# Two attention steps and a normalising stage, moved from stages of their own into the dense passes before them

## The reference, cut to what matters

```python
query, key = (x @ Wq + bq).reshape(n, 2, 128), (x @ Wk + bk).reshape(n, 2, 128)   # 2 heads
qs, ks = query / norm(query), key / norm(key)
terms = [x0]                                        # x, for both heads
for _ in range(4):
    prev = terms[-1]
    gcn = segment_sum(prev[row], col) * deg_inv     # neighbours' mean
    kvs = einsum('lhm,lhd->hmd', ks, prev)
    attn = (einsum('nhm,hmd->nhd', qs, kvs) + prev.sum(0)) / (qs . ks.sum(0) + n)
    terms.append(0.5 * gcn + attn)
x = layernorm(x + (concat(terms) @ Wo + bo) / 2)
```

## Time and profile before

| what | value |
|---|---|
| median of 3 runs (lowest, highest) | 5326.28 us (5324.18, 5327.95) |
| profiled execution, its span | 5325.0 us |
| PE, PEld busy over the span | 81%, 57% |
| DVE, ACT, POOL busy | 53%, 27%, 61% |
| DMA | 909 MB, mean 171 GB/s |
| second dense pass, from 2758.3 us to 3222.0 us | 463.6 us |
| step two, to 3301.6 us | 79.6 us |
| third dense pass, to 3764.2 us | 462.6 us |
| step three, to 3862.3 us | 98.1 us |
| fourth dense pass, to about 4196 us | 334 us |
| normalising stage, to 4279.6 us | 84 us |

### The profile page before, as it was taken

The page is one execution under the profiler, slowest core; times in us unless marked ns, Lnnn a source line. Parts: engine busy times, 40 slices in busy tenths (PEclk is TensorE's granted clock), DMA queues, the critical chain, the costliest instruction groups (busy, mean ns, idle before and its releaser), DMA issues. The chain is left out here.

```text
span 5325.0 us, 78049 instructions
## 1 busy us (share of the span) xinstructions
PE 4321.5 (81%) x26640; PEld 3018.0 (57%) x26640; DVE 2815.1 (53%) x7430; ACT 1451.2 (27%) x2914; POOL 3251.7 (61%) x3382
## 2 busy tenths in 40 slices
PE   4677866979868787788879997999889767777786
PEld 3444434545535556554446664666555467667775
DVE  6588886755367776535562315221432444455554
ACT  1377850010057664111120102010210122222222
POOL 2766626767767775075516661776177367777774
PEclk6789988989989999699989998999999898999998
DMA  4265559999933344195588887988697465555553
GB/s 145 45 61 80 91 100 194 199 182 187 202 80 101 104 126 109 60 289 159 168 265 271 270 248 250 280 268 253 228 303 241 130 171 144 143 149 146 151 153 82
DMA packets 1261118, 909.00 MB, mean 171 GB/s; under 512 B 446403, under 2 KB 1181934, under 8 KB 1260638
## 3 DMA queue, kind: packets, MB, share of 16 engines
q1 hardware_dynamic: 909866, 519.09, 39.3%
q0 software_dynamic: 102704, 232.38, 16.1%
q10 hardware_dynamic: 248132, 152.25, 9.9%
HBM read 696.10 MB, written 118.89 MB: 153 GB/s over the span
## 5 line engine op out<-in xcount | busy, mean ns | idle before, releaser
L1687 PE MATMUL ps<-adj_d,xs_d 128*128 128x464 bf16 (+1 forms) x4704 | 992.8, 367 | 60.1 <-DVE xs_d L1648 60.1
L3166 POOL DMA_INDIRECT rows_mg<-p_tab,src_idx x784 | 758.3, 967 | 273.4 <-issue 238.1
L1601 POOL DMA_INDIRECT rows_d<-xh_tab,src_idx x632 | 617.7, 977 | 479.8 <-POOLq L187 207.4
L1601 POOL DMA_INDIRECT rows_d<-x_tab,src_idx x512 | 499.1, 975 | 475.5 <-POOLq L187 264.4
L1687 PEld LDWEIGHTS ps<-adj_d,xs_d 128*128 128x128 bf16 x4704 | 466.1, 101 | 509.1 <-DVE xs_d L1648 61.9
L1295 POOL DMA_INDIRECT rows_d<-h_tab,slot_idx x490 | 497.0, 1014 | 266.9 <-issue 143.9
L2216 POOL DMA_INDIRECT rows_g<-x_tab,src_idx x444 | 434.2, 978 | 164.7 <-issue 127.3
L3263 PE MATMUL ps<-win_mg,turned_hot_mg 128*128 128x128 f32 x1568 | 341.2, 302 | 201.2 <-DVE pre_mg L3215 201.0
L1431 PE MATMUL ps<-adj_d,xs_d 128*128 128x512 bf16 (+1 forms) x2028 | 441.0, 375 | 54.6 <-DVE xs_d L1396 49.9
L1673 PEld LDWEIGHTS ps<-onehot_d,rows_d 128*128 128x128 f32 x3552 | 428.6, 192 | 66.6 <-DVE onehot_d L1619 33.5
L1673 PE MATMUL ps<-onehot_d,rows_d 128*128 128x72 f32 (+1 forms) x3552 | 421.4, 275 | 31.3 <-DVE onehot_d L1619 26.3
(11 more groups left out here) (442 smaller groups left out, 7541.4 us busy)
## 6 DMA issues: line engine op xcount, KB each, us to landing
adj_d<-adjacency SPq DMA_DIRECT2D x140, 812.0 KB
adj_d<-adjacency SPq DMA_DIRECT2D x84, 857.5 KB
attr_mg<-in_edge_attr SPq DMA_DIRECT2D x195, 256.0 KB
xp_g<-x_tab SPq DMA_DIRECT2D x70, 448.0 KB
k_rows_d<-k_tab ACTq DMA_DIRECT2D x56, 448.0 KB
loc_mg<-loc_rows SPq DMA_DIRECT2D x196, 128.0 KB
q_s<-q_tab SPq DMA_DIRECT2D x42, 448.0 KB
rden_s<-rden_tab SPq DMA_DIRECT2D x42, 448.0 KB
```

The source lines that it names most:

```text
L1601: nc.gpsimd.indirect_dma_start(rows[:, q % GR * K + k, :], None, table, bass.IndirectOffsetOnAxis(ap=src_idx[:, j:j + 1], axis=0)).then_in ...
L1687: last = nc.tensor.matmul(ps[:, m % 2, 0:w], xs[:, g * GW + k, e, :], adj[:, slot, k, 0:w], start=(g == 0 and k == 0 and e == 0), stop=(g ...
L3166: nc.gpsimd.indirect_dma_start(rows[:, q % RR, k, :], None, p_tab, bass.IndirectOffsetOnAxis(ap=src_idx[:, j:j + 1], axis=0)).then_inc(row ...
```

## The change

Steps two and three lose their stages. The pass itself goes through the nodes in 14 **visits** of 512 or 384 columns (`NODE_PARTS`), as soon as the sums of those columns are complete (`needs`). `fused_slots` writes the order: one **slot** for each dense tile, and some behind the last tile, each with at most one piece of `keys_values`, up to two groups, the tile, and a visit (`ask` ahead of the groups on PE, `finish` behind the tile). Pieces come one to a slot from the second slot on, where before one came to five tiles; visits may begin at slot 35. The two passes have 4 blocks a head instead of 5, so 56 tiles instead of 70, and gather 368 tiles of edges (92 groups) instead of 316 (79 groups). By the order, 9 visits stand beside tiles and 5 behind the last one, together with the last 8 groups. All loads and stores of a visit are issued by ACT; the loads of rden and share go into a single buffer, q into two. Buffers are those of `raw` and of the key rows. In pass two ACT first stores the whole `xT` to `x_kept`, for the passes' general fallback (a branch not taken here).

In pass four `ending_slots` puts two pieces into a slot, so `keys_values` and `LastAttention` end at slot 18, and the normalising stage (`LastNodes`, the same work as `layer2_last`) enters a visit at every second tile from slot 19 on; 11 enter beside tiles, 3 behind them, and the last is through 6 slots later. There, too, `xT` is stored to `x_kept` first, and DVE may change `xT` only when that is done.

Cut to its core:

```diff
-SPLITS = {1: Split(6, 490, 528), 2: Split(5, 464, 468)}
+SPLITS = {1: Split(6, 490, 528), 2: Split(4, 464, 416)}
...
+        def fused_slots():
+            slots, visits, ready = [], [], [(c, nw * P) for c, nw in NODE_PARTS]
+            clock, t, q, p, finished = 0.0, 0, 0, 0, 0
+            free_at = order.index((blocks, G - 1)) + 1
+            while t < tiles or q < groups or finished < PARTS_N:
+                took = pieces[p:p + 1] if t else []
+                opens = p >= len(pieces) and t >= free_at
+                p += len(took)
+                group = []
+                while q < groups and len(group) < 2 and clock > 4.5 + GATHER_US * (q + 1):
+                    group.append(q)
+                    q += 1
+                tile = t if t < tiles else None
+                able = [v for v in ready if needs(*v)[1] <= q and (needs(*v)[0] < 0 or stored_at(needs(*v)[0]) < t or tile is None)]
+                ask = finish = None
+                if opens and able:
+                    ask = len(visits)
+                    visits.append(able[0])
+                    ready.remove(able[0])
...
                     def _(pe):
-                        for t in range(tiles + 1):
-                            beside(nc.tensor, t)
-                            for q in gathered[t]:
+                        for s, slot in enumerate(slots):
+                            beside(nc.tensor, slot)
+                            if step:
...
+                                if slot.ask is not None:
+                                    step.ask(pe, slot.ask, finished)
+                            for q in slot.groups:
...
+                            if slot.finish is not None:
...
+                                step.finish(pe, slot.finish, turn_bank(slot))
...
+                def start(self, act):
+                    if keeps:
+                        act.dma_start(x_kept, xT[:, 0:NP]).then_inc(self.kept, 16)
...
+                def load_rest(self, act, i):
...
+                        if i:
+                            act.wait_ge(self.made, HEADS * i)
+                        act.dma_start(self.share[:, 0:w], dinv_row[c:c + w].partition_broadcast(P)).then_inc(self.rest_in, 16)
+                        for h in range(HEADS):
+                            act.dma_start(self.rden[h][:, 0:w], rden_tab[h * P:(h + 1) * P, c:c + w]).then_inc(self.rest_in, 16)
...
+                def ask(self, eng, i, finished=0, again=False):
...
+                        for h in range(HEADS):
+                            nc.tensor.matmul(ps[:, 4 + h, 0:w], kv[:, h, :], self.q[i % 2][h][:, 0:w], start=True, stop=True).then_inc(self.asked, 1)
+                    elif eng is nc.vector:
+                        eng.wait_ge(self.rest_in, 16 * (1 + HEADS) * (i + 1))
...
+                        nc.vector.tensor_tensor(a, a, self.share[:, 0:w].unsqueeze(1).to_broadcast([P, HEADS, w]), ALU.mult).then_inc(self.scaled, 1)
...
+        class LastNodes:
...
+            def begin(self, act, again=False):
...
+                    act.dma_start(x_kept, xT[:, 0:NP]).then_inc(self.kept, 16)
...
+            def on_vector(self, line, ready):
...
+                    dve.wait_ge(self.kept, 16)
+                    nc.vector.tensor_tensor(x, x, a, ALU.add).then_inc(self.final, 1)
...
-            if step < ORDER:
-                layer2_step(step)
-        layer2_last()
+        layer2_step(1)
+        for step, table, to, sums in ((2, xh_tab, xh2_tab, G), (3, xh2_tab, xh_tab, PARTS_N)):
+            make = fused_step(step, to, step == 2)
+            dense_pass(f"2{step}", table, HEADS, SPLITS[HEADS], [[keys_values(table, HEADS, 1, sums)]], make)
...
+        dense_pass(f"2{ORDER}", x_tab, 1, SPLITS[1], [[keys_values(xh_tab, HEADS, 2, PARTS_N)], [LastAttention]], ending=LastNodes)
```

More of the change, by code:

```diff
@@ L45 @@
 BATCH = 14
+NODE_PARTS = [(g * GC + half * BLOCK, GW - BW if half else BW) for g in range(G) for half in range(2)]
+PARTS_N = len(NODE_PARTS)
+Slot = namedtuple("Slot", "pieces groups tile ask finish")
+TILE_US, GROUP_US, GATHER_US, PIECE_US, VISIT_US = 4.2, 1.75, 5.05, 1.6, 4.3
 MOST = 256
@@ L1508, in dense_pass @@
-                    for k, piece in enumerate(pieces):
-                        before = phases[opened.index(k) - 1] if k and k in opened else ()
-                        due[1 + k * (tiles - 1) // len(pieces)].append((before, piece))
-                    gathered = [[] for t in range(tiles + 1)]
-                    for q in range(groups):
-                        gathered[min(tiles, 2 + q * tiles // groups)].append(q)
-                    def beside(eng, t):
-                        for before, piece in due[t]:
+                            for k in range(most):
+                                pieces.append([(work, k, g) for work in phase if work.parts == most] +
+                                              [(work, 0, g) for work in phase if work.parts < most and k == most // 2])
@@ new lines, in dense_pass, with stored_at, needs @@
+                    pieces = [(phases[opened.index(k) - 1] if k and k in opened else (), piece) for k, piece in enumerate(pieces)]
+                    def stored_at(m):
+                        return order.index((m + 1, 2) if m else (1, G - 1)) if m < heads * blocks - 1 else tiles
+                    def needs(c, w):
+                        first_block = (heads - 1) * blocks
+                        covering = [first_block + b for b in range(blocks) if b * block_of < c + w]
+                        g = c // GC
+                        of_dense = c + w <= blocks * block_of
+                        sums = 0 if of_dense else groups if g == G - 1 else max(0, FINAL[g] - tail // K)
+                        return covering[-1] if c < blocks * block_of else -1, sums
@@ new lines, in dense_pass @@
+                    if step:
+                        slots, visits = fused_slots()
+                        step.visit(visits)
+                        begins = min(k for k, slot in enumerate(slots) if slot.ask is not None)
+                    elif last_nodes:
+                        slots, visits = ending_slots()
+                        last_nodes.visit(visits)
+                        begins = min(k for k, slot in enumerate(slots) if slot.ask is not None)
+                    else:
+                        slots = even_slots()
@@ L1518, in beside @@
+                    first_idle = min(k for k, slot in enumerate(slots) if slot.tile is None)
+                    def beside(eng, slot):
+                        for before, piece in slot.pieces:
                             for work in before:
@@ L1638, in add @@
                             nc.vector.tensor_tensor(a, a, sums_of(q), ALU.add).then_inc(added, 1)
[L1640 to L1642 removed]
+                        for k, slot in enumerate(slots):
+                            if slot.tile is not None and splits_at(slot.tile) is not None:
+                                h, g = splits_at(slot.tile)
                                 s = h * G + g
```

683 lines of the change are left out of this document (502 added, 181 removed).

## The result

The changed kernel took **5374.93 us** (median of 4 runs, 5361.89 to 5384.15) against 5325.23 us for the kernel before (4 runs, 5323.53 to 5327.95) in the same session: a ratio of 1.009 (95% interval 1.0077 to 1.0104), so slower by some 50 us. Forecast were 5275 us, 5200 to 5350, with a chance of 0.16 for slower by over 0.2%. The forecast missed its range and its sign. The profiled execution has a span of 5382.4 us; it was the slowest of the four.

What follows compares the result with a forecast made beforehand. PE was taken to bound passes two and three, no engine the three stages. Gains of 131 us made 5325 into 5194; new DMA waits of 81 us left a gain of 50: 5275 us, range 5200 to 5350.

Steps and rivals of the forecast that it cites:

- The sum without new waits: Steps two and three and pass four fused: gains of 50, 46 and 35 us, together 131, giving 5194 us.
- The waits for pieces: PE waiting for the loads of pieces: 15 us each in passes two and three, 17 in pass four.
- the starved queue: Rival: piece loads stay at 84 GB/s on ACT's queue, 91 us a pass, 5427 us; 0.16, shared with waits over 142 us.
- the volume alone: Rival: only bytes count, waits at their floors of 9, 9 and 17 us, 5229 us; chance 0.20.
- the uncovered chain: DVE's part of visits behind the last tile, covered by nothing: 3 us for the first visit, 4 for the last.
- late loads: Visits' `load_rest` into one buffer, 0.79 MB after `made`: 0 to 30 us a pass, 8 taken.
- The passage: From a fused pass's last store to the next stage: 4 us.
- Pass four: With the normalising stage inside: 383 us against 417.8 before waits, gain 35; some 410 us with waits.
- The tiling: Passes two and three with 56 tiles and 92 groups: PE's work 411 us, 35 less a pass.
- The rivals: Only volume counts, 5229 us, 0.20; ACT's queue starves, 5427, shared 0.16; visits behind late gathers, 5300 to 5337, no own chance.
- The slower rival: ACT's queue starves in passes two and three: 91 us of waits each, 5427 us; 0.16, shared with waits over 142 us.
- its point of 40 us a pass: Piece waits in passes two and three from which the slower rival decides: 3.1 us more to a slot.

Runs made afterwards that it cites:

- shifted_back: The changed kernel with 48 words (192 bytes) of each SBUF partition left empty ahead of the planes, no instruction changed: 5360.82 us, ratio 1.0059.
- before_shifted: The kernel before with 80 words (320 bytes) of each SBUF partition left empty ahead of the planes: 5339.58 us, ratio 1.0024.
- pieces_apart: The changed kernel with the 14 pieces of the second and third pass at every second tile, not at each: 5335.29 us, ratio 1.0014.
- q_early: The changed kernel with a visit's q loads given out once PE has asked with the buffer, value sums writing their own buffer: 5366.15 us, ratio 1.0091.
- no_fallback: The changed kernel with pieces at every second tile, early q loads and 48 empty words (5305.82 us), now without the fallback's node work: 5301.0 us, ratio 0.9934.
- five_blocks: The changed kernel with the old tiling, five blocks and 316 gathered tiles in passes two and three: 5394.81 us, ratio 1.0139.
- tiling_only: The kernel before with four blocks and 368 gathered tiles in passes two and three, nothing moved: 5368.12 us, ratio 1.0080.
- little_kept: The changed kernel with both stores of x_kept cut to 1/49 of their bytes: 5360.44 us, ratio 1.0074.
- both_little_kept: The changed kernel with pieces at every second tile, early q loads and 48 empty words (5305.82 us), now x_kept stores at 1/49: 5299.85 us, ratio 0.9934.

## Why the prediction was wrong

The profiled execution lies 107 us above the forecast, the median 100. By stages: the first pass 17, step one and what lies ahead 7, the second pass 35, the third 27, the fourth 20.

Two steps failed. "**The sum without new waits**" put the three moved stages too low: PE at the durations of an undisturbed pass, 50 us behind the last tile where there were 61, 4 us for a passage where there were 8 to 10, and no wait between the ending's pieces. And the first pass was left out of the sum without a reason.

*The first pass: a term that was missing.* "Only what is edited changes" was never written down, but the sum rests on it. The edit moved every buffer of the passes by 704 bytes, which costs 14 us in the first pass by `shifted_back` and 17 by `before_shifted`, 9 by the means of all kernels, and perhaps some in the fourth, 423.5 us in `shifted_back`. The second pass of `shifted_back`, 564.8 us, was not shorter.

*The waits for pieces: right in size; PE's work beside them was not.* Forecast were 15 us a pass plus 8 for `x_kept`; measured 12.8 + 6.7 us in the second pass and 18.2 in the third. DMA was at 0.99, as said, and the starved queue (91 us) and the volume alone (9 us) both fell. The sum priced PE at the durations of an undisturbed pass (4.12, 1.72, 1.56 us). With 9 of 14 visits that is some 436 us up to the end of the last tile of the second pass; PE was busy for 449.7. The clock behind waits is part of that, since `pieces_apart` has 10 us less there, though in the third pass it gave nothing back.

*Behind the last tile.* The sum gave the five visits their share of PE's work (5/14 of 58, 21 us), the eight groups 14, the uncovered chain 3 + 4 and late loads 8: 50 us. It took 61.2. PE's work was 45.4 us and not 35, at a granted clock of 0.80 (the eight groups alone 18 us), and the waits for q 12.7. The loads were late at q and not only at `rden`: in a slot behind the tiles the next q is loaded in the visit before's finish, and needed at once. I had said PE would idle ahead of L3109 for `made`; it idled 0.3 us there and 12.7 us ahead of L3083. Removing it alone brought little, because `rden` is the next in line (`q_early`).

*The passage.* "4 from the last store to the next stage" was read behind a step. As I read the program, a fused pass has at its end both the wait for its last stores and the branch that used to stand between pass and step, and it jumps over longer code (only this part is shown, by `no_fallback`): 9.9, 8.3 and 8.3 us, 14 in all over the forecast.

*Pass four.* The waits for loads (18.5 us against 17) and the chain behind the last tile (28.8 us from its end to the last store, against 26) were right. The sum lacked PE's waits for DVE between dependent pieces of the attention, 9.1 + 3.8 us and more; before, a tile lay between any two. They did not decide, though: spread out, the pass grew by 8 us.

*The tiling* was rightly a gain inside the fused pass: against `five_blocks` 32 us by the two stages, 20 by the medians. The forecast said 35 a pass for PE; its busy time fell by 26, and 10 us of waits behind the tiles came back.

*The rivals.* None of the three was it. The slower rival named one queue and one price; what came was five smaller terms of 5 to 20 us, each too small for its point of 40 us a pass. The chance of 0.16 for their sum was too low: the values taken for the waits lay near the low ends of their ranges (15 us between 9 and 91, 5 between 0 and 17, 8 between 0 and 30), and the work itself had no range at all. The prediction also gave both stages 22 MB of DMA; by the earlier trace rows step three moves 263 GB/s for 98 us, 26 MB.

## What to carry to other kernels

Where a pass is bound by one engine, spread the side work over it at the rate at which its loads come, and not as early as the order allows: one condition on the slot was worth 40 us of the 50 lost. Give a wait of PE a range from its own length to one and a half times that: 18.2 us of waits removed gave 19 in the third pass, 12.8 gave 20 in the second. Time an unchanged stage too: if it is longer at the same share of DMA and fewer GB/s, look at where the buffers came to lie before looking at the instructions.

## What the runs showed of the hardware that I had not expected

- Moving buffers in the SBUF changed what a full DMA brought. In the allocation of the compiled programs the gathered rows of the one-head passes begin on a multiple of 512 bytes before and in `shifted_back`, and 320 bytes behind one in the changed kernel and in `before_shifted`; the rates were 322, 322, 307 and 296 GB/s, the first pass 418, 421, 435 and 435 us. That it is this buffer was not tried, and 512 is not the multiple that it needs: by the sizes of the buffers in the programs, `tiling_only` moves this one by 256 bytes, and it had 322 GB/s too (its line stands below). A multiple of 256 would fit all kernels that ran; no run tests it.
- By the Trainium skill (DMA: Bandwidth & Descriptors, Issuing engines are not separate DMA queues) the transfers of all queues run on the same 16 engines. The trace agrees: with almost no bytes in `x_kept`, a store of ACT's queue, PE's wait of 6.7 us for a tile of SP's queue is gone (`little_kept`, and again in `both_little_kept`).
- Skipped code costs: 8 us over three passages, without one instruction of it run.
- Waits of 4 and 6.75 us are followed by 1.3 to 1.7 us of slower work each, most waits up to 2 us by 0.1, and the five visits behind the last tile ran at a granted clock of 0.80.

The 74 us of the first pass in `tiling_only`:

```profile
2285.30:2359.30 74.00, 71.22 (x470) 49.81 (x468) 25.34 (x91) 8.46 (x10) 56.61 (x58) 1.00 1.11 322
```
